# Layer 7's normalisation and first products moved among the last cells of layer 6, a last GRU update in another form, and all differences of layer 7 on VectorE

## The chip, the cores and the metric

The kernel runs on one core of one Trainium2 chip. The metric is the device time of one execution in microseconds. Engines run their own instruction streams in program order and wait for each other on semaphores: TensorE (PE; its weight loads are PEld), VectorE (DVE), ScalarE (ACT), GpSimd (POOL), SyncE (SP, which issues the transfers).

## The reference

A stack of four blocks over x of 16 x 128 tokens and 128 features. Each block adds two gated parts to x: x = x + tanh(g) * part(layernorm(x)). Six of these eight parts (layers 0 to 5) are not touched: experts, a quantised feed-forward net, block-sparse attention, a composition net, an mLSTM, and an expert-choice net. The last two are:

```python
# layer 6: slots, three iterations; each ends in a GRU cell
for _ in range(3):
    ...                                   # attention over the context gives u
    r = sigmoid(ir + hr); z = sigmoid(iz + hz)
    n = tanh(inn + r * hn)
    slots = (1 - z) * n + z * slots
x = x + tanh(g_xattn[3]) * slots
# layer 7: ternary feed-forward net
scale = mean(|w|); w_t = clip(round(w / scale), -1, 1)
h = gelu(layernorm(x) @ w_t1.T + b1)
x = x + tanh(g_ffn[3]) * (h @ w_t2.T + b2)
```

## The kernel before

x is held transposed in xT, features on the 128 partitions and 2048 tokens in the free dimension, in four chunks c of 512 tokens. PSUM is eight banks of 512 columns. The order of the work is written out by hand, one function per engine and layer (`pe_layer6`, `act_layer6`, `dve_layer6` and so on); what an engine does while another is late is only what stands next in its own function.

**Normalisation.** `pe_norm`, `act_norm` and `dve_norm` take the four chunks in a staggered order. For each chunk TensorE multiplies x by a centring matrix (L251), ScalarE squares it (L267), TensorE takes the mean of the squares (L256), ScalarE forms the inverse root as Ln and Exp (L271, L272) and VectorE multiplies (L280). For layer 7 the result is split in two f16 parts, x16 (L286 and L288). Semaphores: s_x counts chunks of xT, then s_cen, s_sq, s_var, s_rstd, s_norm, s_lo.

**Layer 6.** Its time is seven half steps (`halves`). Half step k runs the attention of two chunks of iteration k // 2 and the GRU cells of the two chunks before them. The cells of half step 5 are those of the last iteration for chunks 0 and 1, the cells of half step 6, in which no attention is left, those for chunks 2 and 3. In a cell VectorE scales the update u (L1672), TensorE runs eight f32 products for the gates r and z of the two chunks (L1611, L1612) and four for n (L1616, L1617), ScalarE takes sigmoids (L1648, L1649), VectorE forms the sum t (L1693, L1694), ScalarE takes tanh (L1652), and VectorE updates the slots: h - n, times z, plus n (L1699 to L1701). In the last iteration it also adds the gated slots to xT (L1704), which counts s_x. A f32 product of 128x512 is two instructions in the trace. ScalarE's tables are loaded for sigmoid and tanh (at L1648) and for Ln and Exp again after tanh (L1654).

**Layer 7.** GpSimd makes the ternary weights early in layer 6 (L1716 to L1718). After the norm of all four chunks TensorE runs for each chunk eight f16 products up (four tiles f of 128 hidden features, two parts of x16; L1737) and eight down (two parts of h16; L1747). ScalarE takes GELU of each tile into h32, f32 (L1760), and for tiles 0 and 1 once more as f16 into h16 (L1762); for tiles 2 and 3 VectorE casts h32 (L1771). The low part of h16 is the difference h32 - h16: GpSimd makes it for tiles 0 and 1 (L1725), VectorE for 2 and 3 (L1772). VectorE ends a chunk with two operations: product plus bias times gate (L1778), and the sum with xT (L1779); SyncE then stores the chunk. h32 has four tiles, one per f, so ScalarE's next GELU of a tile waits for that tile's difference of the chunk before.

## Time and profile before

| what | us |
|---|---|
| median of 3 runs | 910.16 (906.8, 910.16, 913.28) |
| the profiled execution, device time | 919.15 |
| its span, first to last instruction | 917.3 |
| mean granted TensorE clock in it | 0.944 |
| median from issue to landing of a store of a chunk of xT | 2.2 |

The rows further down come from that one profiled execution. A timeline row reads: start from the span's beginning, duration, engine, line of the kernel, operation, output <- inputs, and in brackets the idle time ahead of it with what ended it. Instructions of one kind that follow each other are merged (x8), and the duration is then that of all. PEclk is the granted TensorE clock as a share of full speed. Parts of the chain of waits are in order of time; each piece is what the end of the program waited for at that moment.

### The profile page before, as it was taken

How to read it: one execution, taken by the hardware profiler on the slowest of the kernel's cores; microseconds unless marked ns; L12 is line 12 of the kernel's file. 1: busy time of each engine (PE TensorE's matmuls, PEld its weight loads, DVE VectorE, ACT ScalarE, POOL GpSimd, SP SyncE). 2: the span in 40 equal slices, each digit the busy share in tenths (PEclk: the TensorE clock that was granted, in tenths of full speed). 3: DMA queues.
4: the chain of work that ended last, by engine and by line, in shares of the span. 5: the costliest groups of instructions: out<-in, count | busy, mean ns of one | idle time of the engine just before them, and what ended most of it. 6: DMA issues, size and time to landing. Idle time of an engine off the chain costs nothing.

```text
span 917.3 us, 14682 instructions
## 1 busy us (share of the span) xinstructions
PE 793.4 (86%) x5833; PEld 498.2 (54%) x5833; DVE 619.7 (68%) x980; ACT 568.6 (62%) x984; POOL 287.3 (31%) x253
## 2 busy tenths in 40 slices
PE   6899999998967879999859999958998968888766
PEld 3676777775424545455459555535677844444322
DVE  4986766673567676588686688847775156777476
ACT  4997979894746766445633444445586646666473
POOL 1334333332467775440030311066940020000013
PEclk9999999999979999999959998978999979999898
DMA  7300000006100001110000000060000000000001
GB/s 261 108 24 24 22 22 25 24 25 100 22 15 22 20 24 31 26 31 2 1 0 2 1 1 0 2 232 0 2 1 1 1 0 1 0 1 0 1 0 46
DMA packets 13140, 25.69 MB, mean 28 GB/s; under 512 B 3592, under 2 KB 5264, under 8 KB 12816
## 3 DMA queue, kind: packets, MB, share of 16 engines
q1 hardware_dynamic: 8976, 16.36, 6.2%
q0 software_dynamic: 4096, 8.40, 3.7%
q8 instruction: 46, 0.75, 0.3%
q14 instruction: 22, 0.18, 0.1%
HBM read 23.69 MB, written 1.05 MB: 27 GB/s over the span
## 4 chain that ended last, share of the span: by engine, by line
PE 59%; DVE 19%; ACT 13%; issue 4%; POOL 2%; DMA 1%; another core or an unknown queue 1%; SPq 0%; POOLq 0%; DVEq 0%; ACTq 0%
PE ps L388 9%; PE ps L355 8%; PE ps L942 6%; PE ps L1108 3%; PE ps L1460 2%; PE ps L661 2%; DVE big L1195 2%; PE ps L1430 2%; PE ps L536 2%; ACT big L1177 1%; PE ps L1144 1%; PE ps L1075 1%; PE ps L1616 1%; PE ps L1135 1%; PE ps L1449 1%
## 5 line engine op out<-in xcount | busy, mean ns | idle before, releaser
L1049 POOL DMA_INDIRECT pe<-in_rpe,idx x128 | 134.4, 1050 | 195.9 <-PE ps L388 112.3
L436 DVE TENSOR_TENSOR big<-l1f_w,big 128x512 f16<-128x512 f32 x128 | 87.1, 691 | 42.2 <-ACT big L422 39.2
L421 ACT ACTIVATE l1f_w<-ps,wcols 128x512 f32<-128x512 f32 x128 | 90.4, 707 | 16.1 <-PE ps L355 11.7
L355 PE MATMUL ps<-vx,big 128*128 128x512 f16 x384 | 89.6, 383 | 6.3 <-DVE vx L237 3.4
L388 PEld LDWEIGHTS ps<-big 128*128 128x128 f16 x1536 | 88.3, 98 | 8.6 <-DVE big L436 1.5
L388 PE MATMUL ps<-big 128*128 128x128 f16 x1536 | 91.0, 219 | 0.9 <-DVE big L436 0.9
L422 ACT ACTIVATE big<-ps,wcols 128x512 f16<-128x512 f32 x128 | 91.1, 712 | 0.0
L355 PEld LDWEIGHTS ps<-vx,big 128*128 128x128 f16 x384 | 37.2, 99 | 54.1 <-issue 11.1
L942 PE MATMUL ps<-nT,l1f_w 128*128 128x512 f32 x128 | 57.6, 592 | 0.0
L848 ACT ACTIVATE big<-ps 128x1024 f32<-128x1024 f32 x32 | 32.7, 1023 | 38.5 <-PE ps L658 30.6
L1725 POOL TENSOR_TENSOR big<-l1f_w,big 128x512 f16<-128x512 f32 x8 | 10.5, 1327 | 138.5 <-ACT big L1762 138.5
L1177 ACT ACTIVATE big<-ps,small 128x128 f32<-128x128 f32 x128 | 35.2, 379 | 26.9 <-PE ps L1135 26.9
L661 PE MATMUL ps<-big 32*128 32x512 f16 x192 | 28.2, 399 | 17.9 <-ACT big L848 9.4
L1066 POOL TENSOR_TENSOR big<-nT,consts 128x512 f32<-128x512 f32 x16 | 16.8, 1060 | 83.8 <-PE ps L1125 43.8
L864 DVE TENSOR_REDUCE small<-ps 128x16 f32<-128x1024 f32 x32 | 38.4, 1216 | 5.7 <-PE ps L652 5.7
L969 ACT ACTIVATE big<-ps,wcols 128x1024 f32<-128x1024 f32 x16 | 17.9, 1117 | 39.1 <-PE ps L942 39.1
L1108 PE MATMUL ps<-big,pe 128*128 128x128 f32 x256 | 32.0, 289 | 11.4 <-DVE big L1195 11.2
L1108 PEld LDWEIGHTS ps<-big,pe 128*128 128x128 f32 x256 | 31.4, 205 | 11.7 <-DVE big L1195 11.3
L789 POOL TENSOR_TENSOR big<-big,consts 128x1024 f16<-128x1024 f16 x16 | 30.4, 1904 | 20.6 <-PE ps L652 20.4
L1144 PEld LDWEIGHTS ps<-vx,big 128*128 128x128 f32 x256 | 33.3, 205 | 6.3 <-DVE big L1248 3.8
L942 PEld LDWEIGHTS ps<-nT,l1f_w 128*128 128x128 f32 x128 | 23.2, 190 | 23.9 <-issue 23.9
L1559 DVE TENSOR_TENSOR big<-small,big 128x528 f16<-128x528 f32 x32 | 25.2, 796 | 16.0 <-ACT big L1488 15.9
(351 smaller groups left out, 1834.2 us busy)
## 6 DMA issues: line engine op xcount, KB each, us to landing
big<-in_l0x_w SPq DMA_DIRECT2D x16, 256.0 KB, 3.3
pe<-in_l2f_w SPq DMA_DIRECT2D x16, 256.0 KB, 7.0
pe<-in_rpe,idx POOLq DMA_INDIRECT x128
cT<-in_cT SPq DMA_DIRECT2D x1, 1024.0 KB, 8.2
l1f_w<-in_l1f_w SPq DMA_DIRECT2D x1, 1024.0 KB, 5.1
vx<-in_ctok SPq DMA_DIRECT2D x1, 1024.0 KB, 16.9
out_xT<-xT SPq DMA_DIRECT2D x4, 256.0 KB, 2.2
xT<-in_xT SPq DMA_DIRECT2D x1, 768.0 KB
```

What stands on the lines that cost most here:

```text
L355: mm = te.matmul(bank(f), w16[:, e, a, f * 128:(f + 1) * 128], x16[:, c, b, :], start=(n == 0), stop=(n == 2))
L388: mm = te.matmul(bank(4 + k % 2)[:, t * D:(t + 1) * D], h16[:, k % 2, a, f, t * S:(t + 1) * S], w16[:, k % E, b, F + f * D:F + (f + 1) * D ...
L421: act.activation(h32[:, f, :], bank(f), ACT.Relu, bias=b, scale=1 / W_UP)
L422: act.activation(h16[:, k % 2, 0, f, :], bank(f), ACT.Relu, bias=b, scale=1 / W_UP).then_inc(M0["act"], 1)
L436: dve.tensor_tensor(h16[:, k % 2, 1, f, :], h32[:, f, :], h16[:, k % 2, 0, f, :], SUB).then_inc(M0["lo"], 1)
L661: return te.matmul(bank(4 + t % 2), kT[quad(t), p, tok(b)], qblk1[quad(t), b % QS, r, :, :], start=(part == 0), stop=False)
L864: dve.tensor_reduce(mxp[:, b % 2, 2 * u:2 * u + 2, 0:8], ps[:, 1024 * u:1024 * (u + 1)].rearrange("p (t g k) -> p t g k", t=2, k=BLK), AX, ...
L942: mm = te.matmul(bank(at + r), l1f_w[:, w * D:(w + 1) * D], nT[:, cs(2 * (k // NC) + r)], start=True, stop=True)
L1049: pool.indirect_dma_start(out=pe[:, v * D:(v + 1) * D], out_offset=None, in_=ins["rpe"], in_offset=bass.IndirectOffsetOnAxis(ap=idx[:, v:v ...
L1108: mm = te.matmul(bank(1 + f % 3)[:, j * 128:(j + 1) * 128], peT[:, f * VG + j, :], qblk[:, :, f * VG + j, :], start=True, stop=True)
L1144: mm = te.matmul(bank(6 + b % 2)[:, h * HW2:(h + 1) * HW2], cw[:, b % 2, h, :], vx4[:, b, h, :], start=True, stop=True)
L1177: ins_ = act.activation(dx[:, st % 2, h, :], bank(4 + j)[:, (h % 4) * S:(h % 4 + 1) * S], ACT.Exp, bias=a4[:, g:g + 1])
```

## The change

In the last half step of layer 6 (half step 6) the norm of layer 7 for chunks 0 and 1 is put in on all three engines, and `pe_norm`, `act_norm` and `dve_norm` are not called for layer 7. On TensorE it stands between nothing (there is no attention left) and the cells' eight products; on ScalarE between the inverse of the attention sums and the sigmoids; on VectorE between u and t. Layer 7 on TensorE begins with the up products of chunk 0, then come the norms of chunks 2 and 3, then the loop over chunks, in which the up products of the next chunk stand ahead of the down products of this one. The banks of the up products are 0, 1, 4 and 5, of the down products 6 and 7.

The update of the last iteration takes another form: with gate g, x + g (1 - z) n + g z h. VectorE forms g - g z, then g z h, and adds the latter to xT while n is not needed yet; behind tanh are one product and one sum. These are five operations for a chunk instead of four, two of them behind tanh.

ScalarE's f16 GELU is taken for three tiles instead of two, VectorE casts one, and makes all four differences; GpSimd's part of layer 7 ends with the ternary weights. The gated bias g * b2 is made once, in layer 6, and added to xT for all four chunks ahead of VectorE's first difference, so that a chunk's output is one fused operation from PSUM.

TensorE at the start of the last half step, before. L1622 and L1623 end the attention of half step 5, L1611 and L1612 are the products for r and z:

```order
L1622 MATMUL ps<-big,pe 128x128 x4
L1623 MATMUL ps<-big,ones 128x512
L1611 MATMUL ps<-big 128x512
L1612 MATMUL ps<-nT,big 128x512
L1611 MATMUL ps<-big 128x512
L1612 MATMUL ps<-nT,big 128x512
L1611 MATMUL ps<-big 128x512
```

and in the change (L1657 and L1658 the attention, L244 centring and L248 variance of layer 7's norm, L1646 and L1647 r and z):

```order
L1657 MATMUL ps<-big,pe 128x128 x4
L1658 MATMUL ps<-big,ones 128x512
L244 MATMUL ps<-xT,consts 128x512 x2
L248 MATMUL ps<-nT,consts 128x512 x2
L1646 MATMUL ps<-big 128x512
L1647 MATMUL ps<-nT,big 128x512
L1646 MATMUL ps<-big 128x512
```

Two centring and two variance products stand now ahead of the eight cell products.

TensorE from the products for n into layer 7, before. L1616 and L1617 are those for n, L251 and L256 the norm, L1737 the up and L1747 the down products:

```order
L1616 MATMUL ps<-big 128x512
L1617 MATMUL ps<-nT,big 128x512
L251 MATMUL ps<-xT,consts 128x512 x2
L256 MATMUL ps<-nT,consts 128x512
L251 MATMUL ps<-xT,consts 128x512
L256 MATMUL ps<-nT,consts 128x512
L251 MATMUL ps<-xT,consts 128x512
L256 MATMUL ps<-nT,consts 128x512 x2
L1737 MATMUL ps<-vx,big 128x512 x16
L1747 MATMUL ps<-big 128x512 x8
```

and in the change (L1651 and L1652 n, L244 and L248 the norm, L1779 up, L1798 down):

```order
L1651 MATMUL ps<-big 128x512
L1652 MATMUL ps<-nT,big 128x512
L1779 MATMUL ps<-vx,big 128x512 x8
L244 MATMUL ps<-xT,consts 128x512 x2
L248 MATMUL ps<-nT,consts 128x512 x2
L1779 MATMUL ps<-vx,big 128x512 x8
L1798 MATMUL ps<-big 128x512 x8
```

The up products of chunk 0 stand ahead of what is left of the norm, that of chunks 2 and 3.

VectorE in the last half step, before. L1672 is u, L1693 and L1694 t, L1699 to L1701 the slots, L1704 the sum into xT:

```order
L1672 TENSOR_TENSOR big<-ps,big 128x512 x2
L1693 SCALAR_TENSOR_TENSOR big<-ps,wcols,big 128x512
L1694 TENSOR_TENSOR big<-ps,big 128x512
L1693 SCALAR_TENSOR_TENSOR big<-ps,wcols,big 128x512
L1694 TENSOR_TENSOR big<-ps,big 128x512
L1699 TENSOR_TENSOR big<-nT,big 128x512
L1700 TENSOR_TENSOR big<-big 128x512
L1701 TENSOR_TENSOR nT<-big 128x512
L1704 SCALAR_TENSOR_TENSOR xT<-nT,gt,xT 128x512
```

and in the change, behind u and the parts of layer 7 for chunks 0 and 1, where L1738 and L1739 t, L1743 to L1745 the part of the update ahead of tanh and L1748, L1749 that behind it:

```order
L1738 SCALAR_TENSOR_TENSOR big<-ps,wcols,big 128x512
L1739 TENSOR_TENSOR big<-ps,big 128x512
L1743 TENSOR_SCALAR big<-big,small,gt 128x512
L1744 SCALAR_TENSOR_TENSOR big<-big,gt,nT 128x512
L1745 TENSOR_TENSOR xT<-xT,big 128x512
L1743 TENSOR_SCALAR big<-big,small,gt 128x512
L1744 SCALAR_TENSOR_TENSOR big<-big,gt,nT 128x512
L1745 TENSOR_TENSOR xT<-xT,big 128x512
L1748 TENSOR_TENSOR big<-big 128x512
L1749 TENSOR_TENSOR xT<-xT,big 128x512
L1748 TENSOR_TENSOR big<-big 128x512
L1749 TENSOR_TENSOR xT<-xT,big 128x512
```

The update of the slots is gone; the part ahead of tanh's result is done for both chunks before the part behind it is begun for the first.

```diff
@@ -238,6 +238,34 @@
         def x_done(layer, c):
             return NCH * layer + c + 1 if layer < 2 else 2 * NCH + BC * (c + 1) if layer == 2 else NCH * layer + B - NCH + c + 1
+        def pe_cen(te, i, c, dst):
+            te.wait_ge(s_x, x_done(i - 1, c))
+            te.matmul(dst, centre_w, xT[:, cs(c)], start=True, stop=True).then_inc(s_cen, 1)
+        def pe_var(te, i, c, dst):
+            te.wait_ge(s_sq, NCH * i + c + 1)
+            te.matmul(dst, mean_w, nT[:, cs(c)], start=True, stop=True).then_inc(s_var, 1)
+        def act_square(act, i, c, src):
+            act.wait_ge(s_cen, NCH * i + c + 1)
+            act.activation(nT[:, cs(c)], src, ACT.Square).then_inc(s_sq, 1)
+        def act_rstd(act, link, i, c, src):
+            act.wait_ge(s_var, NCH * i + c + 1)
+            link(act.activation(nT[:, cs(c)], src, ACT.Ln, bias=eps5[:]))
+            act.activation(nT[:, cs(c)], nT[:, cs(c)], ACT.Exp, scale=-0.5).then_inc(s_rstd, 1)
+        def dve_normed(dve, i, c, src):
+            dve.wait_ge(s_rstd, NCH * i + c + 1)
+            dve.tensor_tensor(nT[:, cs(c)], src, nT[:, cs(c)], MUL).then_inc(s_norm, 1)
+        def dve_parts7(dve, c):
+            dve_normed(dve, 7, c, bank(c))
+            dve.wait_ge(s_norm, NCH * 7 + c + 1)
+            dve.tensor_copy(x16[:, c, 0, :], nT[:, cs(c)]).then_inc(s_hi, 1)
+            dve.wait_ge(s_hi, NCH + c + 1)
+            dve.tensor_tensor(x16[:, c, 1, :], nT[:, cs(c)], x16[:, c, 0, :], SUB).then_inc(s_lo, 1)
         def pe_norm(te, i, more=None):
             if i == 4:
@@ -1580,6 +1608,8 @@
         rc4 = sm(2024, BC)
         thr = sm(2028, 8)
+        minus_g6 = sm(2036, 1)
+        g_b2 = sm(2037, 1)
         def halves():
@@ -1605,6 +1635,11 @@
                 for it, c in attend:
...
                     te.matmul(bank(c), mean_w, buf[0][:, cs(c)], start=True, stop=True).then_inc(X6["var"], 1)
+                if half == 2 * ITERS:
+                    pe_cen(te, 7, 0, bank(0))
+                    pe_cen(te, 7, 1, bank(1))
+                    pe_var(te, 7, 0, bank(4))
+                    pe_var(te, 7, 1, bank(5))
                 for it, c in cell:
...
                     for j in range(2):
@@ -1624,12 +1659,17 @@
         def act_layer6(act, link):
             act_norm(act, link, 6)
-            for attend, cell in halves():
+            for half, (attend, cell) in enumerate(halves()):
                 for it, c in cell:
...
                     act.activation(buf[0][:, cs(c)], buf[0][:, cs(c)], ACT.Exp, scale=-1.0).then_inc(X6["rinv"], 1)
+                if half == 2 * ITERS:
+                    act_square(act, 7, 0, bank(0))
+                    act_square(act, 7, 1, bank(1))
+                    act_rstd(act, link, 7, 0, bank(4))
+                    act_rstd(act, link, 7, 1, bank(5))
                 for it, c in attend:
...
                         act.wait_ge(X6["slots"], NCH * (it - 1) + c + 1)
@@ -1654,6 +1694,8 @@
                     act.preload_act_table_set(LN_EXP)
         def dve_layer6(dve, link):
+            link(dve.tensor_scalar(minus_g6, gt[:, 6:7], -1.0, None, MUL))
+            link(dve.tensor_tensor(g_b2, gt[:, 7:8], col("l3f_b2"), MUL))
             dve.tensor_tensor(lnw6, wcols[:, COL_AT["gru_bi"][0]:COL_AT["gru_bi"][0] + 2],
...
             dve_norm(dve, 6)
@@ -1670,6 +1712,9 @@
                 for it, c in cell:
...
                     dve.tensor_tensor(buf[2][:, cs(c)], bank(4 + c), buf[0][:, cs(c)], MUL).then_inc(X6["u"], 1)
+                if half == 2 * ITERS:
+                    dve_parts7(dve, 0)
+                    dve_parts7(dve, 1)
                 for it, c in attend:
                     eb = buf[1][:, cs(c)].rearrange("p (b k) -> p b k", b=BC)
@@ -1692,22 +1737,26 @@
                     dve.wait_ge(X6["g_ps"], NCH * it + c + 1)
...
                     dve.tensor_tensor(bt, bank(c), bt, ADD).then_inc(X6["t"], 1)
-                for it, c in cell:
-                    bt = buf[3][:, cs(c)]
-                    dve.wait_ge(X6["n"], NCH * it + c + 1)
-                    link(dve.tensor_tensor(buf[2][:, cs(c)], nT[:, cs(c)], bt, SUB))
-                    link(dve.tensor_tensor(buf[2][:, cs(c)], buf[2][:, cs(c)], buf[1][:, cs(c)], MUL))
-                    dve.tensor_tensor(nT[:, cs(c)], bt, buf[2][:, cs(c)], ADD).then_inc(X6["slots"], 1)
-                    if it == ITERS - 1:
-                        dve.wait_ge(X6["slots"], NCH * it + c + 1)
-                        dve.scalar_tensor_tensor(xT[:, cs(c)], nT[:, cs(c)], gt[:, 6:7], xT[:, cs(c)], MUL, ADD).then_inc(s_x, 1)
-        t7 = work[:, 4096:4096 + 2 * CW].rearrange("p (r n) -> p r n", r=2)
+                if half >= 2 * ITERS - 1:
+                    for it, c in cell:
+                        dve.wait_ge(X6["t"], NCH * it + c + 1)
+                        link(dve.tensor_scalar(buf[0][:, cs(c)], buf[1][:, cs(c)], minus_g6, gt[:, 6:7], MUL, ADD))
+                        link(dve.scalar_tensor_tensor(buf[2][:, cs(c)], buf[1][:, cs(c)], gt[:, 6:7], nT[:, cs(c)], MUL, MUL))
+                        link(dve.tensor_tensor(xT[:, cs(c)], xT[:, cs(c)], buf[2][:, cs(c)], ADD))
+                    for it, c in cell:
+                        dve.wait_ge(X6["n"], NCH * it + c + 1)
+                        link(dve.tensor_tensor(buf[2][:, cs(c)], buf[3][:, cs(c)], buf[0][:, cs(c)], MUL))
+                        dve.tensor_tensor(xT[:, cs(c)], xT[:, cs(c)], buf[2][:, cs(c)], ADD).then_inc(s_x, 1)
+                else:
+                    for it, c in cell:
+                        bt = buf[3][:, cs(c)]
+                        dve.wait_ge(X6["n"], NCH * it + c + 1)
+                        link(dve.tensor_tensor(buf[2][:, cs(c)], nT[:, cs(c)], bt, SUB))
+                        link(dve.tensor_tensor(buf[2][:, cs(c)], buf[2][:, cs(c)], buf[1][:, cs(c)], MUL))
+                        dve.tensor_tensor(nT[:, cs(c)], bt, buf[2][:, cs(c)], ADD).then_inc(X6["slots"], 1)
+        UP7 = (0, 1, 4, 5)
         def pool_layer7(pool, link):
             pool.wait_ge(F7["thr"], 2)
@@ -1719,64 +1768,70 @@
                 if j == 0:
...
             ins_.then_inc(F7["tern"], 1)
-            for c in range(NCH):
-                for f in range(FT // 2):
-                    pool.wait_ge(F7["act"], FT * c + f + 1)
-                    pool.tensor_tensor(h16[:, c % 2, 1, f, :], h32[:, f, :], h16[:, c % 2, 0, f, :], SUB).then_inc(F7["lo_pool"], 1)
+        def pe_up7(te, c):
+            te.wait_ge(s_lo, NCH + c + 1)
+            te.wait_ge(s_norm, NCH * 7 + 2)
+            for f in range(FT):
+                if c:
+                    te.wait_ge(F7["act"], FT * (c - 1) + f + 1)
+                for p in range(2):
+                    mm = te.matmul(bank(UP7[f]), tern[:, f * 128:(f + 1) * 128], x16[:, c, p, :], start=(p == 0), stop=(p == 1))
+                mm.then_inc(F7["up"], 1)
         def pe_layer7(te):
-            pe_norm(te, 7)
             te.wait_ge(F7["tern"], 1)
-            for c in range(NCH + 1):
-                if c < NCH:
-                    te.wait_ge(s_lo, NCH + c + 1)
-                    for f in range(FT):
-                        if c:
-                            te.wait_ge(F7["act"], FT * (c - 1) + f + 1)
-                        for p in range(2):
-                            mm = te.matmul(bank(f), tern[:, f * 128:(f + 1) * 128], x16[:, c, p, :], start=(p == 0), stop=(p == 1))
-                        mm.then_inc(F7["up"], 1)
-                if c:
-                    k = c - 1
-                    te.wait_ge(F7["lo_pool"], FT // 2 * (k + 1))
-                    te.wait_ge(F7["lo"], FT // 2 * (k + 1))
-                    if k >= 2:
-                        te.wait_ge(s_x, x_done(7, k - 2))
-                    for f in range(FT):
-                        for p in range(2):
-                            mm = te.matmul(bank(4 + k % 2), tern[:, F + f * D:F + (f + 1) * D], h16[:, k % 2, p, f, :],
-                                           start=(f == 0 and p == 0), stop=(f == FT - 1 and p == 1))
-                    mm.then_inc(F7["down"], 1)
+            pe_up7(te, 0)
+            pe_cen(te, 7, 2, bank(2))
+            pe_cen(te, 7, 3, bank(3))
+            pe_var(te, 7, 2, bank(6))
+            pe_var(te, 7, 3, bank(7))
+            for k in range(NCH):
+                if k + 1 < NCH:
+                    pe_up7(te, k + 1)
+                te.wait_ge(F7["lo"], FT * (k + 1))
+                te.wait_ge(s_rstd, NCH * 8)
+                if k >= 2:
+                    te.wait_ge(s_x, x_done(7, k - 2))
+                for f in range(FT):
+                    for p in range(2):
+                        mm = te.matmul(bank(6 + k % 2), tern[:, F + f * D:F + (f + 1) * D], h16[:, k % 2, p, f, :],
+                                       start=(f == 0 and p == 0), stop=(f == FT - 1 and p == 1))
+                mm.then_inc(F7["down"], 1)
         def act_layer7(act, link):
-            act_norm(act, link, 7)
+            act_square(act, 7, 2, bank(2))
+            act_square(act, 7, 3, bank(3))
+            act_rstd(act, link, 7, 2, bank(6))
+            act_rstd(act, link, 7, 3, bank(7))
             for c in range(NCH):
...
                     if c:
-                        act.wait_ge(F7["lo_pool" if f < FT // 2 else "lo"], FT // 2 * (c - 1) + f % (FT // 2) + 1)
+                        act.wait_ge(F7["lo"], FT * (c - 1) + f + 1)
                     if c >= 2:
                         act.wait_ge(F7["down"], c - 1)
-                    ins_ = act.activation(h32[:, f, :], bank(f), ACT.Gelu, bias=col("l3f_b1", f))
-                    if f < FT // 2:
-                        ins_ = act.activation(h16[:, c % 2, 0, f, :], bank(f), ACT.Gelu, bias=col("l3f_b1", f))
+                    ins_ = act.activation(h32[:, f, :], bank(UP7[f]), ACT.Gelu, bias=col("l3f_b1", f))
+                    if f < FT - 1:
+                        ins_ = act.activation(h16[:, c % 2, 0, f, :], bank(UP7[f]), ACT.Gelu, bias=col("l3f_b1", f))
                     ins_.then_inc(F7["act"], 1)
         def dve_layer7(dve, link):
-            dve_norm(dve, 7)
+            dve_parts7(dve, 2)
+            dve_parts7(dve, 3)
+            for c in range(NCH):
+                dve.wait_ge(s_cen, NCH * 7 + c + 1)
+                link(dve.tensor_scalar(xT[:, cs(c)], xT[:, cs(c)], g_b2, None, ADD))
             for c in range(NCH + 1):
                 if c < NCH:
-                    for f in range(FT // 2, FT):
+                    for f in range(FT):
                         dve.wait_ge(F7["act"], FT * c + f + 1)
-                        link(dve.tensor_copy(h16[:, c % 2, 0, f, :], h32[:, f, :]))
+                        if f == FT - 1:
+                            link(dve.tensor_copy(h16[:, c % 2, 0, f, :], h32[:, f, :]))
                         dve.tensor_tensor(h16[:, c % 2, 1, f, :], h32[:, f, :], h16[:, c % 2, 0, f, :], SUB).then_inc(F7["lo"], 1)
                 if c:
-                    dve_out7(dve, link, c - 1)
-        def dve_out7(dve, link, c):
-            dve.wait_ge(F7["down"], c + 1)
-            link(dve.tensor_scalar(t7[:, c % 2, :], bank(4 + c % 2), col("l3f_b2"), gt[:, 7:8], ADD, MUL))
-            dve.tensor_tensor(xT[:, cs(c)], xT[:, cs(c)], t7[:, c % 2, :], ADD).then_inc(s_x, 1)
+                    dve.wait_ge(F7["down"], c)
+                    dve.scalar_tensor_tensor(xT[:, cs(c - 1)], bank(6 + (c - 1) % 2), gt[:, 7:8], xT[:, cs(c - 1)], MUL, ADD).then_inc(s_x, 1)
```

## Rows read from the trace of the kernel before

**Rows 1.** The page, part 1: busy us (share of the span) xinstructions.

```profile
PE 793.4 (86%) x5833; PEld 498.2 (54%) x5833; DVE 619.7 (68%) x980; ACT 568.6 (62%) x984; POOL 287.3 (31%) x253
```

**Rows 2.** Timeline, 854 to 861: start, us, engine, line, operation [idle before].

```profile
854.30 0.68 DVE L1699 TENSOR_TENSOR big<-nT,big 128x512 f32<-128x512 f32 x1
...
855.16 1.28 ACT L1654 ACT_TABLE_LOAD   x1
...
855.28 1.02 PE L1623 MATMUL ps<-big,ones 128*128 128x512 f32 x2
...
856.47 0.75 DVE L1704 SCALAR_TENSOR_TENSOR xT<-nT,gt,xT 128x512 f32<-128x512 f32 x1
...
859.30 0.75 DVE L1704 SCALAR_TENSOR_TENSOR xT<-nT,gt,xT 128x512 f32<-128x512 f32 x1
...
860.71 2.07 PE L1611 MATMUL ps<-big 128*128 128x512 f32 x2 [4.41 <-DVE big L1672]
```

**Rows 3.** The chain of waits: start us, us, what.

```profile
860.71 2.07 PE ps L1611 x2
...
872.91 0.87 PE ps L1617 x2
```

**Rows 4.** Timeline, 875 to 889, the norm of layer 7.

```profile
875.27 0.68 DVE L1699 TENSOR_TENSOR big<-nT,big 128x512 f32<-128x512 f32 x1
...
880.28 0.75 DVE L1704 SCALAR_TENSOR_TENSOR xT<-nT,gt,xT 128x512 f32<-128x512 f32 x1
...
886.33 0.63 ACT L272 ACTIVATE nT<-nT 128x512 f32<-128x512 f32 x1
...
886.97 1.28 ACT L1760 ACT_TABLE_LOAD   x1
...
888.29 1.90 PE L1737 MATMUL ps<-vx,big 128*128 128x512 f16 x8 [2.96 <-DVE nT L280]
...
888.93 0.69 ACT L1760 ACTIVATE l1f_w<-ps,wcols 128x512 f32<-128x512 f32 x1 [0.67 <-PE ps L1737]
```

**Rows 5.** Timeline, 891 to 915, layer 7 (891.23: three activations back to back).

```profile
891.23 1.86 ACT L1760 ACTIVATE l1f_w<-ps,wcols 128x512 f32<-128x512 f32 x3
...
899.32 0.69 ACT L1760 ACTIVATE l1f_w<-ps,wcols 128x512 f32<-128x512 f32 x1 [3.04 <-PE ps L1737]
...
900.78 1.89 PE L1747 MATMUL ps<-big 128*128 128x512 f16 x8
...
904.48 3.14 POOL L1725 TENSOR_TENSOR big<-l1f_w,big 128x512 f16<-128x512 f32 x2 [1.50 <-ACT big L1762]
...
905.43 1.28 ACT L1760 ACTIVATE l1f_w<-ps,wcols 128x512 f32<-128x512 f32 x2
...
909.80 3.27 PE L1747 MATMUL ps<-big 128*128 128x512 f16 x8 [2.76 <-issue]
...
913.95 0.69 DVE L1779 TENSOR_TENSOR xT<-xT,big 128x512 f32<-128x512 f32 x1
```

**Rows 6.** Stretches: us, busy of each engine (instructions), PEclk, DMA.

```profile
859.00:865.50 6.50, 4.79 (x6) 2.18 (x7) 2.22 (x4) 1.32 (x2) 0.00 (x0) 0.50 0.00 0
866.00:875.00 9.00, 9.00 (x23) 3.87 (x21) 2.53 (x4) 3.25 (x5) 0.00 (x0) 1.00 0.00 0
880.00:882.50 2.50, 2.50 (x4) 1.01 (x3) 2.40 (x5) 1.38 (x3) 0.00 (x0) 0.50 0.00 0
888.30:893.20 4.90, 4.24 (x16) 1.16 (x16) 2.29 (x4) 4.27 (x8) 2.31 (x2) 1.00 0.00 0
897.00:899.50 2.50, 2.50 (x7) 0.82 (x6) 2.43 (x5) 0.18 (x1) 0.00 (x0) 0.50 0.00 0
```

**Rows 7.** Groups by line on VectorE, whole span: count | busy us, mean ns.

```profile
L1704 DVE SCALAR_TENSOR_TENSOR xT<-nT,gt,xT 128x512 f32<-128x512 f32 x4 | 3.0, 752 | 0.1
...
L286 DVE CAST vx<-nT 128x512 f16<-128x512 f32 x4 | 1.7, 427 | 0.1
...
L1771 DVE CAST big<-l1f_w 128x512 f16<-128x512 f32 x8 | 6.2, 778 | 4.9 <-ACT l1f_w L1760 4.9
```

2 lines of the change are left out of this document (1 added, 1 removed).

## The prediction

> **What bounds the kernel now.** I read the page first. TensorE is busy for 86% of the span and no other engine reaches 70% [rows 1], but that is an average over eight layers, and the change touches only the last 60 us, so everything below is read from the timeline and the chain of waits of that stretch. The reader is to see three things there.
>
> First, the end of the slot layer is one chain over all engines. In the last half step but one, VectorE runs four operations per chunk from 854.30 to 860.06, then the two products that make the updates u, and only then does TensorE start the last cells, at 860.71, after 4.41 us of idleness [rows 2]. From there TensorE is the chain until 873.78 (four gate products of 0.86 a pair close it); then come the gates' ends on VectorE and ScalarE, and the four operations per chunk again, until xT of chunk 3 is done at 881.03 [rows 3, 4].
>
> Second, between xT of chunk 3 and the first GELU at 888.93 lie 7.90 us: the rest of layer 7's normalisation, the table load and the first up products [rows 4].
>
> Third, the GELU run is ScalarE's, 24 activations from 888.93 to 906.71, with one stall of 3.04 us on TensorE. After its last activation 7.93 us more pass before VectorE's last addition ends at 914.64: GpSimd's two differences (3.14 us), VectorE's own two pairs, which stand behind the output of chunk 2, then the down products (3.27 us), then two additions [rows 5].
>
> Through all of it runs TensorE's granted clock. After each long pause the rows show it at 0.50, which is 1.2 GHz, and back at 1.00 (2.4 GHz) only after 3 to 5 us of work: 0.50 from 859.0 to 865.5, 0.50 at 880.0 to 882.5 and at 897.0 to 899.5, against 1.00 at 866 to 875 and, although the pause ahead of it was 2.96 us, at 888.3 to 893.2 [rows 4, 6]. A 128x512 f32 product (two instructions) takes 0.86 us at the high level and about twice that, 1.71, at the low one (the first pair of the cells 2.07). Counted back from 873.78 by four of 0.86 to 870.34, the eight cell products fill 9.63 us from 860.71, where 8 x 0.86 is 6.9 [rows 3].
>
> **The change, term by term.** Each term has two ends: H with the clock high, L with the clock low for about as long after each pause as the rows of before show it.
>
> 1. Last update of chunks 0 and 1. Before, four operations per chunk: 854.30 to 860.06. Now five. The product (1-z)g is a one-input operation on f32 in SBUF. No row has exactly this shape; the bounds are 0.43 us (the cast, one input of the same width in SBUF) and 0.75 (the form with two inputs) [rows 7]. I take 0.43, since the cast is the nearer in kind. Then 0.75 + 0.70 for the fused product and the addition: with the 0.02 to 0.03 us between operations 1.91 per chunk, 3.82 for both, then four additions or products of 0.70 or less for the part behind tanh. x of chunk 0 is ready at 854.30 + 5.25 = 859.55 (before 857.2), of chunk 1 at 860.88 (before 860.06). So the "shorter" update is longer here by 0.8 us: tanh's result is there at 855.14, when the table load after it starts [rows 2], and VectorE is the one that is late. The u products end 0.8 later too, but TensorE has other work there now. The 0.8 stands inside the start times of term 2 and is not added again.
>
> 2. Four products of layer 7 in front of the cells. TensorE runs centre 0, centre 1, variance 0, variance 1 before the eight cell products, in order, and whatever waits there holds the cells. H: centre 0 at 859.6, centre 1 at 860.9 when x is there, variance 1 waits for its Square (ends 862.5), cells from 863.5, eight in 6.9: 870.4, as before (870.34), since the low clock is not paid. Term: 0. L: 859.6, then 1.71 each to about 866.1 (high again at 865.6), cells until 873.0, gates until 876.4. Term: +2.6. ScalarE's two Ln and Exp pairs end near 867.5 and the sigmoid table is loaded by 868.8, before the first gate products are complete (869.5), so they are hidden; if the clock is high, the gates are ready at 867.0 and the table at about 866.2, still hidden. VectorE's six operations for parts 0 and 1 lie where it idles now while TensorE is the chain, and cost nothing.
>
> 3. Last update of chunks 2 and 3: before 875.27 to 881.03 = 5.76; now 6.58 by the count of term 1. Term: +0.8. x of chunk 3 is ready at 881.9 (H) to 884.4 (L).
>
> 4. From x of chunk 3 to the first GELU: before 7.90. The first eight up products are issued before, and only two chunks are left to normalise. H: centre 3 1.0, then variance 2 and 3 to 2.7, Ln 3 behind Exp 2 at 3.2, 0.70 + 0.63, then the GELU table 1.28: 5.8. L: centre 3 starts 0.4 late behind centre 2, all at 1.71 until the clock returns: 7.6. Term: -2.1 to -0.3. The table load was covered by VectorE's splitting before (the first GELU waited 0.67 us for TensorE after it); now nothing covers it, and I have counted it. The row shows the table load at 1.28 us, starting as the Exp before it ends and followed by the next activation at once [rows 4]. By the Trainium skill ("ScalarE: Activation LUTs", What ACT_TABLE_LOAD costs) a drain comes on top, about 2.66 us in all; by that the sum would be 1.4 us worse. This trace does not agree, and I go by the row.
>
> 5. The GELU run. VectorE takes all differences, ScalarE casts three of four itself: 28 activations instead of 24. Three back to back take 1.86 us [rows 5], 0.585 from start to start: 27 x 0.585 + 0.70 = 16.5, against 17.8 before. VectorE has per chunk four differences, one cast and the output, about 3.9 us, under ScalarE's 4.1; the casts took 0.78 on average with GpSimd running beside them and 0.43 without [rows 7], and GpSimd has nothing left here. TensorE has 16 products of 0.215 = 3.4 us a chunk at the high clock and 6.9 at the low one. H: no stall, term -1.3. L: the pause ahead of this run lowers the clock, the down products of chunk 0 take 3.4, the first up product of chunk 2 comes 2.2 us late at ScalarE (before 3.04 at the same place). Term: +0.9. The four additions of the bias (4 x 0.45) stand ahead of VectorE's first difference and make the down products of chunk 0 0.5 late, which is in that figure.
>
> 6. After the last GELU: cast 0.43, difference 0.69, issue 0.05, eight down products 1.89 (H, as those at 900.78) or 3.27 (L, as now), one fused output 0.75 [rows 5, 7]: 3.85 to 5.2, against 7.93. Term: -4.1 to -2.7. This is the surest gain: GpSimd's end, the queue of VectorE behind the output of chunk 2 and the second addition all go.
>
> Two tiny operations at the start of layer 6 lie in VectorE's wait for a variance: 0.
>
> Sum of terms 2 to 6, H: 0 + 0.8 - 2.1 - 1.3 - 4.1 = -6.7. L: 2.6 + 0.8 - 0.3 + 0.9 - 2.7 = +1.3. I expect neither end: a pause of 4.41 us was followed by 6.5 us at the low level and one of 2.96 by none [rows 2, 4, 6]. Of the pauses now, the first is 3.3 us (from 856.30, where the products end, to 859.6), the second about 5, the third about 4. I take the middle, **-2.7 us**. Against the profiled execution's own 919.15 this is 916.45; that execution lies 1% above the median of the runs, 910.16, and taken from the median it gives **907.5**.
>
> **The rivals.**
> - A, forecast: the clock is low in some of the stretches, -2.7 +- 2: 905.5 to 909.5. 56%.
> - B, the overlap gives nothing back: TensorE goes low in each pause as before, so the cells run 2.6 us later and only the tail gains, which the longer updates eat: 0 to +1.3, 910.2 to 911.5. For it: three of the low stretches of before follow such pauses [rows 6]. Against it: the first pause is shorter. 24%.
> - C, the clock stays high nearly everywhere: -5 to -6.7, 903.5 to 905. It needs the new pause of 5 us to leave no mark. 15%.
> - D, slower: the last layer stays at the low level. With only two up products per 1.15 us between the first GELUs, TensorE is not full, and if the clock does not return, its 6.9 us a chunk pass ScalarE's 4.1: +2.8 for each of three chunks, less the 2.2 already counted, on top of L: about +7.5, 917.7. It decides once the low level lasts beyond the up products of chunk 2. Against it: before, the same products brought the clock back within 4.3 us (low at 897.0 to 899.5, high at 900.78, where eight take 1.89 again). 3%.
> - E, the change does not do what it says, and the cells are also held by something that the rows do not show (a semaphore of x that comes with the second update only): like B with another microsecond, 912.5. 2%.
>
> **How the numbers follow.** The likeliest case gives 907.5. A and C with most of B make the range: 903.5 to 911. The three runs shown lie between 906.8 and 913.3, so less than 1% (9.1 us) is no change that a measurement of this kernel can tell. Faster by over 1% would need less than 901.1, below even C's end: 5%, for scatter and for a gain that I do not see. Slower by over 1% needs more than 919.3: D and scatter, 3%. The rest, 92%, is within.
>
> **What would show it.** Right: the last differences and the down products follow the last GELU within 1.3 us, and the last VectorE operation ends 3.9 to 5.2 us after it; GELUs 0.585 apart with at most one stall, before chunk 2; x of chunk 1 about 0.8 us later relative to the gates than now; cells starting 863 to 866.5 on the scale of before, not 860.7; the first GELU between 887.7 and 892.0. Wrong: a fused update near 0.43 us or a one-input product at 0.75 (each moves two chunks twice, up to 1.3 us); casts still at 0.8 us without GpSimd; the low level through chunks 1 to 3; or a table load with a drain of its own.

## The result and the profile after

The changed kernel is a little slower: 913.85 us in the median of 20 runs (911.14 to 917.5) against 911.38 for the kernel before in 20 runs (906.8 to 915.31), ratio 1.0029 with a 95% interval of 1.0015 to 1.0043. I had forecast 907.5 and a range of 903.5 to 911.

The two profiled executions (919.15 before, 912.44 after) do not show this difference as they stand: up to the last sum t of half step 5, where the code is the same but for two tiny operations, they already lie 9.50 us apart (853.69 and 844.19), and in all profiles of this case that point lies between 844.2 and 861.0. So I compare the stretch from that point (the start of VectorE's second L1694 operation of half step 5, L1739 in the change; below it is called the anchor) to the end of the span. It is 63.61 us before and 66.31 after: +2.70, the size of the measured ratio. To set a row of after beside one of before, add 9.50. The two starting points, before and after:

```profile
853.69 0.69 DVE L1694 TENSOR_TENSOR big<-ps,big 128x512 f32<-128x512 f32 x1
...
844.19 0.69 DVE L1739 TENSOR_TENSOR big<-ps,big 128x512 f32<-128x512 f32 x1
```

The last update of chunks 0 and 1 and the start of the cells, in the timeline of the changed kernel (start, us, engine, line, operation, idle before); they answer [rows 2]:

```profile
844.80 0.54 DVE L1743 TENSOR_SCALAR big<-big,small,gt 128x512 f32<-128x512 f32 x1
...
845.38 0.75 DVE L1744 SCALAR_TENSOR_TENSOR big<-big,gt,nT 128x512 f32<-128x512 f32 x1
...
849.70 0.69 DVE L1749 TENSOR_TENSOR xT<-xT,big 128x512 f32<-128x512 f32 x1
...
850.45 3.78 PE L244 MATMUL ps<-xT,consts 128*128 128x512 f32 x4 [3.65 <-DVE xT L1749]
...
854.02 2.98 PE L248 MATMUL ps<-nT,consts 128*128 128x512 f32 x4
...
856.84 1.02 PE L1646 MATMUL ps<-big 128*128 128x512 f32 x2
```

x of chunk 1 is ready at 851.72, which is 861.22 on the scale of before (860.06 there). The cells' first product starts at 856.84, or 866.34, where it was 860.71. Ahead of it now stand two centring products (3.78 us together) and two variance products (2.98), after a pause of 3.65 us. They run at half rate, but for the last half of the last one.

The chain of waits behind it (start, us, what), to [rows 3]:

```profile
857.00 0.86 PE ps L1646 x2
...
866.44 0.87 PE ps L1652 x2
```

Once the cells have begun they run at the high rate: twelve products of 0.86 without a gap to 867.31, or 876.8 on the scale of before, where the same point was 873.78.

The timeline from the update of chunks 2 and 3 to the first GELU, to [rows 4]:

```profile
868.80 0.54 DVE L1743 TENSOR_SCALAR big<-big,small,gt 128x512 f32<-128x512 f32 x1
...
874.45 3.78 PE L244 MATMUL ps<-xT,consts 128*128 128x512 f32 x4 [5.42 <-DVE xT L1749]
875.03 0.69 DVE L1749 TENSOR_TENSOR xT<-xT,big 128x512 f32<-128x512 f32 x1
...
881.93 0.63 ACT L257 ACTIVATE nT<-nT 128x512 f32<-128x512 f32 x1
...
882.58 1.28 ACT L1814 ACT_TABLE_LOAD   x1
...
883.88 0.69 ACT L1814 ACTIVATE l1f_w<-ps,wcols 128x512 f32<-128x512 f32 x1
```

VectorE's update takes from 868.80 to 875.72, 6.92 us (before 5.76); TensorE idles 5.42 us over it. From x of chunk 3 to the first GELU pass 8.16 us (before 7.90), although half of the norm is done.

The GELU run and the tail, to [rows 5]:

```profile
885.29 4.11 PE L1779 MATMUL ps<-vx,big 128*128 128x512 f16 x8 [4.34 <-ACT big L1816]
...
890.04 3.60 PE L1798 MATMUL ps<-big 128*128 128x512 f16 x8 [0.64 <-DVE big L1831]
...
894.24 0.69 ACT L1814 ACTIVATE l1f_w<-ps,wcols 128x512 f32<-128x512 f32 x1 [2.15 <-PE ps L1779]
...
899.66 1.90 PE L1798 MATMUL ps<-big 128*128 128x512 f16 x8 [0.61 <-DVE big L1831]
...
901.66 0.78 ACT L1814 ACTIVATE l1f_w<-ps,wcols 128x512 f32<-128x512 f32 x1
...
903.71 3.34 PE L1798 MATMUL ps<-big 128*128 128x512 f16 x8 [2.15 <-DVE big L1831]
...
907.09 0.75 DVE L1834 SCALAR_TENSOR_TENSOR xT<-ps,gt,xT 128x512 f32<-128x512 f32 x1 [2.77 <-PE ps L1798]
```

The run lasts 18.56 us (before 17.78). ScalarE waits 2.15 us for TensorE ahead of chunk 2, at the same place as before (3.04 there). Behind the last GELU (which ends at 902.44) 5.40 us pass (before 7.93), of them 3.34 in the last down products, all but their first 0.3 us at half rate.

The stretches of the changed kernel (us, busy time of each engine with its instructions, granted clock, DMA), to [rows 6]:

```profile
849.50:856.20 6.70, 5.75 (x7) 2.39 (x8) 3.35 (x6) 1.46 (x4) 0.00 (x0) 0.50 0.00 1
857.00:869.00 12.00, 12.00 (x33) 4.98 (x31) 6.53 (x11) 6.15 (x10) 0.00 (x0) 1.00 0.00 0
874.00:880.50 6.50, 6.05 (x8) 2.39 (x8) 1.69 (x3) 1.72 (x3) 0.00 (x0) 0.53 0.00 0
884.00:893.30 9.30, 7.19 (x16) 1.85 (x17) 8.70 (x16) 8.09 (x14) 0.00 (x0) 0.50 0.00 0
894.00:903.90 9.90, 7.14 (x32) 2.75 (x31) 7.37 (x13) 8.21 (x14) 0.00 (x0) 1.00 0.14 54
904.00:907.00 3.00, 3.00 (x8) 0.79 (x6) 0.31 (x1) 0.00 (x0) 0.00 (x0) 0.50 0.23 87
```

The clock is at 0.50 ahead of and nearly to the end of the four moved products, again over the norm of chunks 2 and 3, for 9 us of the GELU run, and in the last down products. Over the whole stretch its mean is 0.79, against 0.86 before.

VectorE's groups in the changed kernel (count, busy us, mean ns), to [rows 7]:

```profile
L1744 DVE SCALAR_TENSOR_TENSOR big<-big,gt,nT 128x512 f32<-128x512 f32 x4 | 3.0, 751 | 0.1
L1834 DVE SCALAR_TENSOR_TENSOR xT<-ps,gt,xT 128x512 f32<-128x512 f32 x4 | 3.0, 747 | 3.2 <-PE ps L1798 3.2
...
L1743 DVE TENSOR_SCALAR big<-big,small,gt 128x512 f32<-128x512 f32 x4 | 2.2, 541 | 0.1
L1824 DVE TENSOR_SCALAR xT<-xT,small 128x512 f32<-128x512 f32 x4 | 1.9, 485 | 0.1
...
L1830 DVE CAST big<-l1f_w 128x512 f16<-128x512 f32 x4 | 1.7, 421 | 0.0
```

The new one-input product L1743 takes 0.541 us, not the 0.43 that I took; the cast without GpSimd beside it takes 0.421 (0.778 before).

### The profile page after: what moved, and what is told of

Same layout as the page of the kernel before. It is cut to its first block, busy times and chain, and to the rows that moved or that the text cites. A ratio compares the mean times of both kernels' runs of the same rounds, so it can differ in the third digit from the quotient of the medians.

```text
span 910.5 us, 14694 instructions
## 1 busy us (share of the span) xinstructions
PE 798.1 (88%) x5833; PEld 499.3 (55%) x5833; DVE 622.4 (68%) x990; ACT 570.3 (63%) x988; POOL 279.9 (31%) x245
## 3 DMA queue, kind: packets, MB, share of 16 engines
HBM read 23.69 MB, written 1.05 MB: 27 GB/s over the span
## 4 chain that ended last, share of the span: by engine, by line
PE 63%; DVE 21%; ACT 12%; issue 3%; DMA 0%; POOL 0%; SPq 0%; ACTq 0%; DVEq 0%
PE ps L416 9%; PE ps L383 8%; PE ps L970 6%; PE ps L1136 3%; PE ps L689 3%; PE ps L1488 2%; DVE big L1223 2%; PE ps L1458 2%; PE ps L716 2%; PE ps L564 2%; PE ps L702 2%; ACT big L1205 1%; PE ps L706 1%; PE ps L1103 1%; PE ps L1172 1%
## 5 line engine op out<-in xcount | busy, mean ns | idle before, releaser
L1077 POOL DMA_INDIRECT pe<-in_rpe,idx x128 | 136.8, 1069 | 192.0 <-PE ps L416 106.1
L1172 PE MATMUL ps<-vx,big 128*128 128x17 f32 x256 | 32.1, 268 | 3.1 <-DVE big L1276 3.1
L817 POOL TENSOR_TENSOR big<-big,consts 128x1024 f16<-128x1024 f16 x16 | 30.8, 1931 | 12.9 <-PE ps L680 12.8
```

The lines of the kernel that those rows point to most:

```text
L1077: pool.indirect_dma_start(out=pe[:, v * D:(v + 1) * D], out_offset=None, in_=ins["rpe"], in_offset=bass.IndirectOffsetOnAxis(ap=idx[:, v:v ...
L1172: mm = te.matmul(bank(6 + b % 2)[:, h * HW2:(h + 1) * HW2], cw[:, b % 2, h, :], vx4[:, b, h, :], start=True, stop=True)
```

## The experiments

All of them are read by the same five pieces of that stretch: **a** from the start of the last sum t of half step 5 to the start of that of half step 6; **b** on to the end of x of chunk 3; **c** to the first GELU; **d** to the end of the last GELU; **e** to VectorE's last end (the store of 2.6 to 2.7 us follows). "Clock" is the mean granted clock of the stretch.

| kernel | a | b | c | d | e | stretch | clock | ratio to before (95%) |
|---|---|---|---|---|---|---|---|---|
| before | 20.97 | 6.37 | 7.90 | 17.78 | 7.93 | 63.61 | 0.86 | 1 |
| changed | 24.00 | 7.53 | 8.16 | 18.56 | 5.40 | 66.31 | 0.79 | 1.0029 (1.0015 to 1.0043) |
| y_after, changed again | 23.96 | 7.53 | 8.15 | 18.55 | 5.40 | 66.29 | 0.79 | 1.0029 (1.0005 to 1.0053) |
| x_fill, changed, products in 4 pauses | 21.72 | 7.54 | 5.97 | 16.73 | 3.96 | 58.60 | 1.00 | 0.9927 (0.9901 to 0.9952) |
| z_p1, in the 1st pause | 21.72 | 7.53 | 7.67 | 16.73 | 4.37 | 60.69 | 0.88 | one run |
| z_p2, in the 2nd pause | 24.00 | 7.54 | 5.97 | 17.94 | 3.96 | 62.04 | 0.89 | one run |
| x_oldupd, old update | 20.56 | 6.36 | 8.14 | 17.09 | 3.96 | 58.77 | 0.88 | 0.9949 (0.9922 to 0.9977) |
| z_mix, old update in half step 5 | 20.56 | 7.53 | 8.12 | 18.39 | 5.56 | 62.78 | 0.84 | one run |
| x_noovl, no overlap | 21.87 | 7.53 | 9.14 | 16.29 | 5.47 | 62.97 | 0.84 | 0.9978 (0.9950 to 1.0005) |
| x_tail, new tail alone | 20.98 | 6.37 | 7.90 | 16.31 | 5.46 | 59.68 | 0.89 | 0.9927 (0.9902 to 0.9951) |
| y_beffill, before, products in 4 pauses | 18.48 | 6.36 | 6.67 | 17.78 | 6.28 | 58.22 | 0.95 | 0.9969 (0.9942 to 0.9996) |
| y_oldfill | 20.55 | 6.37 | 5.97 | 18.42 | 3.96 | 57.89 | 0.97 | 0.9965 (0.9942 to 0.9988) |
| y_earlyfill | 21.90 | 3.34 | 6.86 | 16.72 | 3.96 | 55.45 | 1.00 | 0.9934 (0.9907 to 0.9962) |
| z_earlynoovl | 19.83 | 3.35 | 9.37 | 16.28 | 3.96 | 55.50 | 1.00 | 0.9920 (0.9888 to 0.9951) |

The pieces of the changed kernel repeat within 0.04 us from one profile to the other. The ratios carry the noise of the 850 us ahead of the stretch; their intervals reach 0.2 to 0.3% to either side, about 2 to 3 us (0.14% in the comparison of 20 runs). The pieces come from one profile of each kernel (two of the changed one).

**x_fill: keep TensorE busy in the pauses.** TensorE gets 16 unused products into free banks, 4, 6, 4 and 2 in its four pauses; nothing reads them. "High clock" below means 1.00 in the profile's rows, "half rate" means 0.50.

```diff
+        def fill(te, dst, n):
+            for _ in range(n):
+                te.matmul(dst, mean_w, consts[:, 0:512], start=True, stop=True)
...
                 if half == 2 * ITERS:
+                    te.wait_ge(X6["t"], NCH * (ITERS - 1) + 2)
+                    fill(te, bank(4), 4)
                     pe_cen(te, 7, 0, bank(0))
...
             pe_up7(te, 0)
+            te.wait_ge(X6["t"], NCH * (ITERS - 1) + 4)
+            fill(te, bank(6), 6)
...
             pe_var(te, 7, 3, bank(7))
+            te.wait_ge(s_rstd, NCH * 7 + 3)
+            fill(te, bank(6), 4)
...
+                if k == NCH - 1:
+                    fill(te, bank(2), 2)
                 te.wait_ge(F7["lo"], FT * (k + 1))
```

> The changed kernel with unused f32 products of 128x512 on TensorE in its four pauses: 4 ahead of the norm of chunks 0 and 1, 6 after the up products of chunk 0, 4 after the last variance, 2 ahead of the last down products. Theory C (clock): the change loses because each pause sends TensorE to the low level, and the four moved products and everything behind them then run at half rate. Then with the clock kept high the cells start about 2.6 us earlier, the norm of chunks 2 and 3 ends about 2 earlier, the 2.15 us stall before chunk 2 is gone and the last down products take 1.9 instead of 3.3: about 8 us less than the changed kernel, ratio to before about 0.994. Theory P (place): the products cost where they stand, whatever the clock: no more than 2 us less than the changed kernel, ratio 1.000 to 1.003, since the cells still wait for centre, Square and variance.

Measured: 7.71 us less than the changed kernel in the stretch and 5.01 less than before, ratio 0.9927. Work was only added, so the cost removed is that of the half rate. It lies in all four places: a -2.28, c -2.19, d -1.83, e -1.44. TensorE's timeline, products of two instructions each:

```profile
862.25 3.60 PE L244 MATMUL ps<-consts 128*128 128x512 f32 x8
866.06 1.13 PE L248 MATMUL ps<-xT,consts 128*128 128x512 f32 x2 [0.22 <-DVE xT L1755]
867.39 1.13 PE L248 MATMUL ps<-xT,consts 128*128 128x512 f32 x2 [0.20 <-DVE xT L1755]
868.36 1.98 PE L252 MATMUL ps<-nT,consts 128*128 128x512 f32 x4
870.17 1.02 PE L1652 MATMUL ps<-big 128*128 128x512 f32 x2
```

Four unused products (3.60 us), then centring 1.13 each and two variances in 1.98. With the clock high the moved products wait for x, 0.2 us each, and the cells start at 870.17, 10.37 us after the anchor at 859.80; in the changed kernel it was 12.65. The stretches of the same kernel:

```profile
862.00:870.00 8.00, 7.58 (x17) 2.81 (x17) 6.33 (x10) 4.86 (x8) 0.00 (x0) 1.00 0.00 1
886.00:893.00 7.00, 6.22 (x13) 1.95 (x13) 3.44 (x6) 3.03 (x5) 0.00 (x0) 1.00 0.00 0
896.00:905.00 9.00, 6.42 (x27) 2.25 (x27) 8.45 (x16) 8.66 (x16) 0.00 (x0) 1.00 0.00 0
914.00:918.00 4.00, 0.93 (x5) 0.20 (x3) 0.75 (x1) 0.00 (x0) 0.00 (x0) 1.00 0.35 131
```

The clock is 1.00 in each. Theory C holds in its place and size. What the moved products cost when the clock is high is a second question; y_beffill and y_oldfill below answer it.

**z_p1 and z_p2: one pause at a time.** The diff is that of x_fill with only the first, or only the second, of its insertions.

> The changed kernel with the unused products in its first pause alone (4, ahead of the norm of chunks 0 and 1). If each pause pays for itself: the stretch from the last sum t of half step 5 to that of half step 6 takes 21.7 us as with all unused products, not 24.0, and everything behind it stays as in the changed kernel, 42.3 us: 64.0 in all. If the low level is one state that the first pause starts, the later stretches shorten too, towards 58.6.

> The changed kernel with the unused products in its second pause alone (6, behind the up products of chunk 0). If each pause pays for itself: 24.0 us to the last sum t, 7.5 to x of chunk 3, 6.0 instead of 8.2 to the first GELU, then 18.6 and 5.4 as in the changed kernel if the third pause lowers the clock by itself, 64.1 in all; 62.2 if it doesn't.

Measured, one profile each: z_p1 60.69, z_p2 62.04. Each takes exactly its own piece back (a 21.72; c 5.97), and both do more: with the first pause filled c, d and e are shorter by 0.49, 1.83 and 1.03 too, so the sum is 5.62 us, not 2.3. With the second filled d loses another 0.62 and e 1.44. So filling one pause changes where the clock falls later; why it falls where it does, these runs do not show. "Each pause pays for itself" fails as an exact rule, and so does the rival that the first starts one state for all: z_p1 still has a mean clock of 0.88 (c 7.67 instead of 5.97, e 4.37 instead of 3.96).

**x_oldupd: undo the update.** The block for `half >= 2 * ITERS - 1` is taken out, and the four old operations are back.

```diff
-                if half >= 2 * ITERS - 1:
-                    for it, c in cell:
-                        dve.wait_ge(X6["t"], NCH * it + c + 1)
...
+                    link(dve.tensor_tensor(buf[2][:, cs(c)], nT[:, cs(c)], bt, SUB))
+                    link(dve.tensor_tensor(buf[2][:, cs(c)], buf[2][:, cs(c)], buf[1][:, cs(c)], MUL))
+                    dve.tensor_tensor(nT[:, cs(c)], bt, buf[2][:, cs(c)], ADD).then_inc(X6["slots"], 1)
+                    if it == ITERS - 1:
+                        dve.wait_ge(X6["slots"], NCH * it + c + 1)
+                        dve.scalar_tensor_tensor(xT[:, cs(c)], nT[:, cs(c)], gt[:, 6:7], xT[:, cs(c)], MUL, ADD).then_inc(s_x, 1)
```

> The changed kernel with the last update as before (four operations, slots written, then the sum into xT); overlap and tail as changed. Theory U (update): the five-operation form costs 1.2 us in either of its two places, so this runs 1.2 to 2.4 us faster than the changed kernel, ratio to before 1.000 to 1.002; in the profile x of chunk 0 stands 2.4 us earlier, the first centring product with it, and from the last sum t to x of chunk 3 pass 5.8 us instead of 6.9. Rival: the update is hidden or neutral, ratio as the changed kernel, 1.003.

Measured: ratio 0.9949, stretch 58.77, 7.54 us less than the changed kernel. Theory U named the right part and gave it a third of its size. VectorE's own time is as expected (b -1.17). The rest is the clock. TensorE's timeline at the same place:

```profile
864.61 1.12 PE L244 MATMUL ps<-xT,consts 128*128 128x512 f32 x2 [0.97 <-DVE xT L1749]
867.46 1.12 PE L244 MATMUL ps<-xT,consts 128*128 128x512 f32 x2 [1.72 <-DVE xT L1749]
868.42 1.98 PE L248 MATMUL ps<-nT,consts 128*128 128x512 f32 x4
870.23 1.02 PE L1646 MATMUL ps<-big 128*128 128x512 f32 x2
```

x of chunk 0 now comes early, so the pause ahead of the first centring product is 0.97 us instead of 3.65, then 1.72 ahead of the second: TensorE does not go to the low level here, both variances take 1.98 together, and the cells start 9.20 us after the anchor instead of 12.65. The new update did not only take 1.17 us more; it held back x of chunk 0, because it does all three early operations of both chunks first. Of the 7.54 us, 3.44 lie in a, 1.17 in b, 1.47 in d and 1.44 in e. In e the pause ahead of the last down products is as long as in the changed kernel, 2.15 us, and they take 1.90 instead of 3.34:

```profile
914.45 1.90 PE L1790 MATMUL ps<-big 128*128 128x512 f16 x8 [2.15 <-DVE big L1823]
```

The same holds in z_p2 (2.14 us, e 3.96). What a pause of this length is followed by depends on more than its length.

**z_mix: the old update in half step 5 alone** (the condition is `half == 2 * ITERS`, and the old branch sums into xT in its last iteration).

> The changed kernel with the old update in half step 5 alone; the new one stays in half step 6. If the update costs in half step 5 by making TensorE's first pause longer (from about 1 to 3.65 us): 20.6 us from sum t to sum t instead of 24.0, of which only 1.2 to 2.4 is VectorE's own time; 7.5 to x of chunk 3 and 8.2 to the first GELU as changed. If the pause is not what counts, 22 or more.

Measured: a 20.56, b 7.53, c 8.12; stretch 62.78. As the pause theory said: of 3.44 us in a, x_fill and y_oldfill (21.72 and 20.55, both at high clock) give 1.17 to VectorE, and 2.27 are the half rate. What the update costs in half step 6, with a alike, is seen against x_oldupd: 4.01 us, 1.17 of it in b, the rest in d and e.

**x_noovl and x_tail: take the overlap away; then the update too.** x_noovl drops the insertions in half step 6 and calls the norms as before; x_tail has the old update besides, so that only the tail is new.

```diff
-                if half == 2 * ITERS:
-                    pe_cen(te, 7, 0, bank(0))
...
+            pe_norm(te, 7)
             te.wait_ge(F7["tern"], 1)
             pe_up7(te, 0)
-            pe_cen(te, 7, 2, bank(2))
...
```

> The changed kernel without the overlap: the norm of layer 7 for all four chunks after the slots, as before; new update and new tail kept. Theory P (place): the four products ahead of the cells cost 3.0 us and give nearly nothing back behind x of chunk 3, so this is 2 us faster than the changed kernel, ratio to before about 1.001; the cells start 1.2 us later than before by the update alone. Rival: the overlap gives back behind the slots what it costs, and without it the stretch from x of chunk 3 to the first GELU is 2 to 3 us longer than in the changed kernel: ratio 1.003 or more.

> The kernel before with the new tail alone: all differences on VectorE, three f16 GELUs on ScalarE, gated bias added ahead, one fused output; up products on banks 0, 1, 4, 5 and the down products behind the next chunk's up products. No overlap, old update. Theory: of the change's parts this is the one that gains, GELU run +0.8 us at most and 2.5 less behind the last GELU: 1.7 to 3 us faster than before, ratio 0.997 to 0.998. Rival: the 28 activations and the four bias additions eat it, ratio 1.000.

Measured: x_noovl 62.97 and 0.9978, x_tail 59.68 and 0.9927. The tail alone gives 3.93 us in the stretch: d -1.47 and e -2.47. Its ratio says more than that (its interval begins at 4.5 us); I leave the difference open. Of the expectation the gain behind the last GELU held, and "28 activations cost 0.8" did not: the stall before chunk 2 is gone there. x_noovl met neither of its expectations. The stretch is 3.34 us shorter than in the changed kernel, where 2 were expected: a is 2.13 shorter, c 0.98 longer (the rival said 2 to 3), and d is 2.27 shorter, which neither theory had. Putting the pieces on one another in the profiles: tail -3.93, then the update +3.29, then the overlap +3.34, which is the +2.70 of the whole. With the old update the overlap goes the other way: x_oldupd is 0.91 us below x_tail. At the clock that these four kernels had, the overlap cost 3.34 us on top of the new update and gained 0.91 on top of the old one. Of that gain 0.72 us lie in d and e, where the clock fell in other places (d +0.78, e -1.50).

**y_after and y_beffill.** The changed kernel again, and the kernel before with 5, 2, 3 and 3 unused products in its pauses.

```diff
+                if half == 2 * ITERS:
+                    te.wait_ge(X6["t"], NCH * (ITERS - 1) + 2)
+                    fill(te, bank(4), 5)
                 for it, c in cell:
                     te.wait_ge(X6["u"], NCH * it + c + 1)
...
+                    if i == 7 and c == 1:
+                        te.wait_ge(X6["t"], NCH * (ITERS - 1) + 4)
+                        fill(te, bank(6), 2)
...
+            pe_norm(te, 7, lambda te, c: c == NCH - 1 and fill(te, bank(7), 3))
+            te.wait_ge(s_norm, NCH * 8)
...
+                    if k == NCH - 1:
+                        fill(te, bank(7), 3)
```

> The changed kernel once more, beside the others on the same chip. If the loss is its own and not that of one chip: ratio to before 1.001 to 1.005; from the last sum t of half step 5 to the end of the span 65 to 66.5 us and 23 to 28 us at the low level in it. Rival: the result depends on when the clock falls, and this profile shows 62 to 64 us with less than 20 us low.

> The kernel before with unused f32 products in its own pauses: 5 ahead of the last cells, 2 behind the centring of chunks 0 and 1, 3 behind the last variance, 3 ahead of the last down products. Theory C (clock): the kernel before pays for the low level too, but less than the changed one (19.5 us low against 27.3 in the profiles): 2.4 us at the cells, 2 to 3 at the stall before chunk 2, 1.4 at the last down products, so 4 to 6 us less than before, ratio 0.994 to 0.996, and 57.5 to 59.5 us from the last sum t of half step 5 to the end. Rival: only long pauses of the changed kernel matter: ratio 1.000.

Measured: y_after has the same ratio and the same pieces. y_beffill: 58.22, 5.39 us less than before, ratio 0.9969, weaker than expected; its interval reaches to 0.9942, which is 5.3 us. The pieces are a -2.49, c -1.23 and e -1.65; in d, where 2 to 3 us were expected, nothing was gained, since the clock fell there all the same. (The 19.5 us low of before in its expectation counted past the end of the span; by the mean clock of 0.86 over 63.61 us it is about 17.8, and 27.8 in the changed kernel.) The kernel before paid for the clock as well, but less.

**y_oldfill, y_earlyfill, z_earlynoovl: the parts at high clock.** y_oldfill is x_oldupd with 1, 4, 4 and 2 unused products. y_earlyfill has the old update for chunks 0 and 1 and 1, 3, 4 and 2 unused products; for chunks 2 and 3 it moves the operations that need only z ahead of the sums t:

```diff
+                if half == 2 * ITERS:
+                    for it, c in cell:
+                        keep, part = cT[:, cs(c)], cT[:, cs(c - 2)]
+                        dve.wait_ge(X6["rz"], NCH * it + c + 1)
+                        link(dve.tensor_scalar(keep, buf[1][:, cs(c)], minus_g6, gt[:, 6:7], MUL, ADD))
+                        link(dve.scalar_tensor_tensor(part, buf[1][:, cs(c)], gt[:, 6:7], nT[:, cs(c)], MUL, MUL))
+                        link(dve.tensor_tensor(xT[:, cs(c)], xT[:, cs(c)], part, ADD))
                 for it, c in cell:
                     bt = buf[3][:, cs(c)]
...
-                        link(dve.tensor_tensor(buf[2][:, cs(c)], buf[3][:, cs(c)], buf[0][:, cs(c)], MUL))
+                        link(dve.tensor_tensor(buf[2][:, cs(c)], buf[3][:, cs(c)], cT[:, cs(c)], MUL))
```

z_earlynoovl is the same without the overlap, with 5, 2, 3 and 2 unused products.

> Overlap and new tail with the old update, and unused products in the pauses: 1, 4, 4 and 2. With the clock high in all of it, what is left against the changed kernel with unused products (58.6 us in this stretch) is the update alone: theory U says 2.3 us less, 56.3; if the update's whole cost was the pauses that it makes longer, the same 58.6. Ratio to before 0.990 to 0.993 in the first case.

> Overlap and new tail; update of chunks 0 and 1 old; for chunks 2 and 3 the three operations that need only z (1-z times g, g z h, sum into xT) stand ahead of the sums t, into free buffers, where VectorE waits for TensorE; two operations are left behind tanh. Unused products 1, 3, 4 and 2. The new form pays where it stands in an idle stretch: from the last sum t to x of chunk 3 about 3.5 us instead of 5.8, t itself up to 1.2 later, so 55 us in the stretch and a ratio of 0.989 to 0.992. Rival: VectorE is full there and t is later by as much as the end is shorter: the same as with the old update.

> As the version with the early part of the update, the new tail and unused products, but the norm of layer 7 behind the slots as before, not among them; unused products 5, 2, 3 and 2. With the clock high everywhere the overlap itself is tested: the cells start earlier (18.5 us and 1.4 for the early part to the last sum t, 19.9 against 21.9), and from x of chunk 3 to the first GELU it takes 6.7 to 7.5 instead of 6.9. So without the overlap about 54 us in the stretch against 55.5, ratio to before 0.988 to 0.993. Rival: with high clock the overlap gives back what it takes: 55.5 or more.

Measured: y_oldfill 57.89 instead of 56.3: 1.17 less than x_fill in a and in b, as theory U says, but its clock still fell once in the GELU run (mean 0.97; d 18.42 instead of 16.73). Its ratio, 0.9965, says less than its 5.72 us. y_earlyfill: 55.45 and 0.9934. VectorE in it:

```profile
872.38 0.55 DVE L1744 TENSOR_SCALAR cT<-big,small,gt 128x512 f32<-128x512 f32 x1 [0.64 <-ACT big L1695]
...
875.89 0.55 DVE L1744 TENSOR_SCALAR cT<-big,small,gt 128x512 f32<-128x512 f32 x1 [1.45 <-ACT big L1695]
...
877.98 0.75 DVE L1751 SCALAR_TENSOR_TENSOR big<-ps,wcols,big 128x512 f32<-128x512 f32 x1
...
880.15 0.69 DVE L1752 TENSOR_TENSOR big<-ps,big 128x512 f32<-128x512 f32 x1
...
882.80 0.69 DVE L1757 TENSOR_TENSOR xT<-xT,big 128x512 f32<-128x512 f32 x1
```

The three early operations of chunk 2 start at 872.38 and those of chunk 3 at 875.89, in what was idle time; the last sum t starts at 880.15 and x of chunk 3 ends at 883.49, 3.34 us on, where it was 6.37. The sum t itself is 1.35 us later than in y_oldfill. That is 1.68 us gained in a and b. But c is 6.86 instead of 5.97, so that up to the first GELU only 0.79 us are left; the rest of the 2.44 us to y_oldfill is d, 1.70, where the clock fell in y_oldfill and not here. Part of the longer c is of the experiment's own making: the three unused products run until 883.58, while x of chunk 2 is there at 882.17.

```profile
880.90 2.84 PE L244 MATMUL ps<-consts 128*128 128x512 f32 x6 [1.26 <-DVE big L1752]
...
883.58 1.88 PE L248 MATMUL ps<-xT,consts 128*128 128x512 f32 x4
```

z_earlynoovl: 55.50 where 54 was expected. Against y_earlyfill the overlap costs 2.07 us in a, gives 2.51 back in c and loses the rest in d. That is the rival's answer, but up to 0.9 us of y_earlyfill's c may be the unused products, so a gain of that size by the overlap is not excluded in this pair.

With the old update the same question has a clearer answer, from y_beffill (no overlap) and y_oldfill (overlap), both at high clock up to the first GELU: a 18.48 and 20.55, b 6.36 and 6.37, c 6.67 and 5.97. The overlap costs 2.07 us in a and gives 0.70 back in c, 1.37 net, with no half rate in it. So theory P was right too, in part. The 24.00 us of a in the changed kernel add up: 18.48 with neither, 2.07 for the moved products at high clock, 1.17 for the new update, 2.28 for the half rate.

The early part of the update has the same test without the overlap: a, b and c are 31.51 us in y_beffill (old update) and 32.55 in z_earlynoovl. It gains 3.01 in b, and loses 1.35 in a, because the sums t come later, and 2.70 in c, because there the norm on ScalarE, which starts only after tanh and its table load, is late and not x. So the new form is worth 0.79 us with the overlap and costs 1.04 without it. A version without the overlap and with the old update, the new tail and unused products was not run; from y_beffill's a to c, z_earlynoovl's d and e and the store it comes to about 54.5 us, an estimate. Both y_earlyfill and z_earlynoovl run faster than the kernel before, but x_tail with far less code has 0.9927, and among x_fill, x_tail, y_earlyfill and z_earlynoovl the intervals do not choose.

## Why the prediction was wrong

1. *Last update of chunks 0 and 1.* Right in direction: the new form is longer there. Mis-sized: L1743 takes 0.541, not 0.43, which makes 0.22 us of the difference; x of chunk 1 is 1.16 us later instead of 0.8. And I priced it at its length alone ("The 0.8 stands inside the start times of term 2"), where it also made a pause of 3.65 us in front of TensorE; x_oldupd has 0.97 there and no low stretch.
2. *Four products in front of the cells.* Forecast 0 to +2.6, measured +3.03 in a, beyond the L end. At high clock the products cost 2.07 where they stand and the new update 1.17, the half rate 2.28, and against them stands the 2.49 of half rate that before paid here. The H end of 0 was sound for the old update (20.56 against 20.97 before). The L end left out the update's 1.17, which I had put "inside the start times": x comes later by it, and so does all behind it.
3. *Last update of chunks 2 and 3.* Forecast +0.8, measured +1.16: of the 0.36 more, 0.22 are the two L1743, the rest the gaps between the operations, which I had counted short.
4. *From x of chunk 3 to the first GELU.* Forecast -2.1 to -0.3, measured +0.26. The H end is met when the clock is high (5.97, forecast 5.8). At low clock it was 8.16, not 7.6: the two centring products took 3.78 back to back, x of chunk 3 being there (875.72) before the first had ended, and the second variance ended at 880.94, which is 5.2 us behind x of chunk 3, not 4.5. The table load cost 1.28, and the next activation followed 0.02 us later (882.58 + 1.28, then 883.88). The rows of before that I had quoted were weaker than I said: there 0.68 us passed after the load, spent waiting for TensorE.
5. *The GELU run.* Forecast -1.3 to +0.9, measured +0.78; at high clock 16.73, with -1.05 near the H end.
6. *The tail.* Forecast -4.1 to -2.7, measured -2.53; at high clock 3.96, forecast 3.85.

The step that failed is the choice after the sum: "I expect neither end ... I take the middle". With -2.7 it put most of the half rate at nothing. The changed kernel lies beyond the L end in five of six terms and near it in the GELU run; the L sum was +1.3, itself 1.4 short, and the kernel is at +2.70. The H end exists too: x_fill is at -5.01 where H said -6.7; of the 1.7 between them 0.75 is in a and 0.37 in b, where the update is. I had named rival B with 24% ("goes low in each pause as before"), and its range ended at 911.5; on a median of 911.38 it would have read about 911.4 to 912.7, still short of 913.85. The evidence for B was in the trace of before, and I read it too narrowly: "a pause of 4.41 us was followed by 6.5 us at the low level and one of 2.96 by none". The last down products of before stood behind a pause of 2.76 us and took 3.27, where eight take 1.89 at the high clock [rows 5], and two more short pauses were followed by the low level (879.50 to 882.80 and 896.60 to 899.80 show 0.50):

```profile
878.07 1.13 PE L256 MATMUL ps<-nT,consts 128*128 128x512 f32 x2 [2.59 <-ACT nT L267]
...
895.64 2.78 PE L1747 MATMUL ps<-big 128*128 128x512 f16 x8 [2.47 <-DVE big L1772]
```

So four of the five pauses over 2.4 us in that stretch were followed by it, and the one of 2.96 was the exception. All three pauses that I had counted for the change (3.3, about 5, about 4 us) were longer than these three short ones; B deserved more than the middle. But length alone does not decide either: the 2.96 us left no mark, and 2.15 us ahead of the last down products were followed by the low level in the changed kernel and not in x_oldupd. What decides it in such cases stays open here. For one and the same kernel it repeats: y_after has the low stretches of the changed kernel at the same places.

Rival D (low through all chunks) did not happen: the clock was back by 894.

## What to carry to other kernels

An overlap that moves products of a serial chain in front of other products costs their time there, 2.07 us here even at the high clock, and gives back only what they had cost behind (0.70). Price both ends before the clock comes in. Then count each pause ahead of TensorE work in the new order, set it beside the pauses of the old trace and the rate behind them, and take the sum at half rate where it is as long as the shorter ones that were followed by it, even if one such pause was not. Filling the pauses with unused products took 5.4 us off the kernel before and 7.7 off the changed one; such products must end before the data that TensorE waits for arrives. A "shorter" form with more operations cost 1.17 us behind the sums t in either place. Moved into idle time ahead of them it took 3.0 off the time behind t, but the time to the first GELU fell by 0.79 in one order and rose by 1.04 in the other: follow a gain to the next thing that waits before it is counted.

## What the runs showed of the hardware

- A one-input f32 operation on VectorE with two per-partition scalars took 0.541 us for 128x512, one with a single such scalar 0.485 (both in SBUF), the cast 0.421 to 0.428.
- A pause of 0.97 us followed by one of 1.72 left TensorE at the high level (x_oldupd); after pauses of 3.65, 5.42 and 4.34 us it was at the low one (changed kernel). In the trace of before it was at the low one after pauses of 4.41, 2.76, 2.59 and 2.47 us, and at the high one after 2.96. After 2.15 us it was at the low one in the changed kernel and at the high one in x_oldupd.
- The stretches of low clock in the changed kernel came at the same places in two profiles taken on different occasions, and its pieces agree within 0.04 us, while the time up to the anchor differed by 12.8 us (844.19 and 857.01).
